# Storing q, k and v from ScalarE's queue in the first tiles of a fused attention layer

## The reference

```
xn = layernorm(x)
q, k, v = xn @ wq + bq, xn @ wk + bk, xn @ wv + bv      # 16 heads of 16
fq, fk = elu(q) + 1, elu(k) + 1
kv    = einsum('bhnd,bhne->bnde', fk, v)      # per row: summed over its 16 heads
k_sum = fk.sum over heads
attn  = einsum('bhnd,bnde->bhne', fq, kv) / (einsum('bhnd,bnd->bhn', fq, k_sum) + 1e-6)
x1 = x + attn @ wo + bo
out = x1 + gelu(layernorm(x1) @ fc_w + fc_b) @ proj_w + proj_b
```

## Time and profile before

| what | value |
|---|---|
| median of 3 runs | 701.37 us (699.54 to 701.44) |
| profiled execution, time | 700.69 us |
| profiled execution, span | 699.0 us |
| TensorE busy | 655.5 us, 94% of the span |
| VectorE busy | 503.0 us, 72% |
| ScalarE busy | 448.0 us, 64% |
| mean granted TensorE clock | 0.975 of full speed |

### The profile page before, as it was taken

How to read it: one execution, slowest core, us unless ns; L and a number is a source line. 1 busy time by engine, 2 the same in 40 slices (tenths; PEclk the granted TensorE clock), 3 DMA queues, 4 the chain that set the end, 5 groups by cost and what they waited for, 6 DMA issues and landing times.

```text
span 699.0 us, 17818 instructions
## 1 busy us (share of the span) xinstructions
PE 655.5 (94%) x6346; PEld 574.9 (82%) x6346; DVE 503.0 (72%) x1350; ACT 448.0 (64%) x895; POOL 369.8 (53%) x535
## 2 busy tenths in 40 slices
PE   7789999998789999999999999999999995899997
PEld 5569999975578898888888888888987772799997
DVE  7874756424578777868878778878766567799992
ACT  5676655513367787767767667776753663788882
POOL 5153664125456545465583764846545563357642
PEclk9879999999999999999999999999999995999999
DMA  7399897414766555544555455564442523567840
GB/s 263 112 296 315 276 304 256 144 46 111 108 105 105 95 78 91 103 85 72 109 82 121 83 89 129 70 113 89 87 82 40 180 92 92 172 218 219 246 161 30
DMA packets 284802, 95.60 MB, mean 137 GB/s; under 512 B 213988, under 2 KB 281664, under 8 KB 284714
## 3 DMA queue, kind: packets, MB, share of 16 engines
q1 hardware_dynamic: 267610, 82.27, 48.7%
q0 software_dynamic: 4992, 11.47, 5.9%
q10 hardware_dynamic: 12112, 0.72, 1.1%
HBM read 65.09 MB, written 29.40 MB: 135 GB/s over the span
## 4 chain that ended last, share of the span: by engine, by line
PE 55%; DVE 7%; issue 4%; POOL 4%; ACT 3%; SPq 2%; DMA 1%; ACTq 1%; POOLq 0%; DVEq 0%
PE bank L1932 49%; PE bank L1941 6%; POOL hids L901 2%; SPq L440 1%; DMA qkv_rows<-feats 1%; DVE den L1765 1%; DVE hn_ L1810 1%; DVE att_ L1763 1%; DMA keys<-qkv_rows 1%; DVE ots L1756 1%; DVE kv_ L1790 1%; POOL sth L886 0%; ACT feats L1125 0%; ACT L1201 0%; POOL stz L870 0%
## 5 line engine op out<-in xcount | busy, mean ns | idle before, releaser
L1932 PE MATMUL bank<-down_w,hids 128*128 128x256 f32 x768 | 104.5, 284 | 1.8 <-POOL hids L901 1.7
L1932 PE MATMUL bank<-hnts,up_w 128*128 128x512 f32 (+1 forms) x432 | 106.0, 382 | 0.1
L901 POOL TENSOR_TENSOR hids<-hid,hids 128x512 fp32r<-128x512 f32 (+1 forms) x68 | 83.3, 1226 | 36.0 <-ACT hids L1177 35.8
L1932 PEld LDWEIGHTS bank<-down_w,hids 128*128 128x128 f32 x768 | 96.6, 188 | 4.8 <-POOL hids L901 3.1
L1932 PE MATMUL bank<-qkv_w,xnts 128*128 128x256 f32 (+1 forms) x384 | 78.3, 352 | 1.5 <-DVE xnts L1776 0.9
L1932 PEld LDWEIGHTS bank<-hnts,up_w 128*128 128x128 f32 x432 | 71.2, 189 | 10.3 <-ACT hids L1177 0.3
L1932 PEld LDWEIGHTS bank<-qkv_w,xnts 128*128 128x128 f32 x384 | 61.7, 192 | 18.9 <-issue 5.8
L867 POOL TENSOR_SCALAR stz<-stz 128x1 f32<-128x1 f32 x32 | 7.2, 226 | 121.6 <-DVE stz L1794 121.6
L1172 ACT ACTIVATE hid<-bank,cols 128x512 f32<-128x512 f32 (+1 forms) x72 | 45.7, 640 | 39.4 <-PE bank L1932 38.0
L1932 PE MATMUL bank<-a_w,xa_h 128*128 128x256 f32 x256 | 60.2, 379 | 0.0
L1932 PE MATMUL bank<-xa_xt,a_w 128*128 128x256 f32 x384 | 55.1, 294 | 0.9 <-DVE xa_xt L1460 0.9
(11 more groups left out here) (292 smaller groups left out, 1562.1 us busy)
## 6 DMA issues: line engine op xcount, KB each, us to landing
qkv_rows<-feats SPq DMA_DIRECT2D x32, 384.0 KB, 3.1
a_raw<-in_L_ffn_w_dram SPq DMA_DIRECT2D x32, 256.0 KB
a_w<-in_L_ffn_w_dram SPq DMA_DIRECT2D x32, 256.0 KB
b_raw<-in_L_ffn_w_dram SPq DMA_DIRECT2D x32, 256.0 KB
b_w<-in_L_ffn_w_dram SPq DMA_DIRECT2D x32, 256.0 KB
mid_rows<-x_all SPq DMA_DIRECT2D x8, 512.0 KB
values<-qkv_rows SPq DMA_DIRECT2D x32, 128.0 KB
late_rows<-x_ SPq DMA_DIRECT2D x8, 512.0 KB, 3.1
```

Source lines behind the costliest of these rows:

```text
L901: pool.tensor_tensor(hids[1][u % 3][:, 0:w], hid[u % 2][:, 0:w], f32(hids[0][u % 3][:, 0:w]), ALU.subtract).then_inc(s_hidl, 1)
L1932: return pe.matmul(dst, left, right, start=start, stop=stop, skip_group_check=True)
```

## The change

ScalarE's queue issues the store of q, k and v for tiles 0 to 6, right behind its copy of v and behind a wait for the features; SyncE keeps the stores of the others. Step 6 joins the steps in which `qkv` stands ahead of `sum_kv` on TensorE, and on ScalarE ahead of `copy_kvt` and `help_keys`; `help_keys` stands ahead of `qkv` from step 7 instead of step 6.

```diff
-        QKV_FIRST = (4, 5)
+        QKV_FIRST = (4, 5, 6)
         HELPED = 7
+
+        def store_grids(engine, n):
+            i, rows = n % 2, slice(n * P, (n + 1) * P)
+            engine.wait_ge(s_feat, n + 1)
+            engine.wait_ge(s_val, n + 1)
+            engine.dma_start(qkv_rows[:, rows, :].rearrange("c p d -> p c d"),
+                             feats[i][:].rearrange("p (c d) -> p c d", c=3)).then_inc(s_grid[i], 16)
...
-            def store_grids(n):
-                i, rows = n % 2, slice(n * P, (n + 1) * P)
-                sp.wait_ge(s_feat, n + 1)
-                sp.wait_ge(s_val, n + 1)
-                sp.dma_start(qkv_rows[:, rows, :].rearrange("c p d -> p c d"),
-                             feats[i][:].rearrange("p (c d) -> p c d", c=3)).then_inc(s_grid[i], 16)
...
             for s in range(MID_STEPS):
-                if at(s, 2) is not None:
-                    store_grids(s - 2)
+                if at(s, 2) is not None and s - 2 >= HELPED:
+                    store_grids(sp, s - 2)
...
-                if 6 <= s < HELPED + 3:
+                if QKV_FIRST[-1] < s < HELPED + 3:
                     help_keys(s - 3)
                 if at(s, 2) is not None:
                     qkv(s - 2)
+                    if s - 2 < HELPED:
+                        store_grids(act, s - 2)
...
                 elif at(s, 5) is not None:
                     sum_att(s - 5)
+                if s == 6:
+                    qkv(4, v_free)
+                    v_free = (s_val, 5)
                 if at(s, 4) is not None:
                     sum_kv(s - 4)
```

## The result

| kernel | median, us | runs | ratio to before | 95% interval |
|---|---|---|---|---|
| before | 701.59 | 6 | 1 | |
| after | 706.08 | 6 (704.15 to 706.58) | 1.0049 | 1.0026 to 1.0072 |

The change makes the kernel 0.49% slower, 3.4 us by the ratio (1.8 to 5.0 by its interval); the two medians differ by 4.5 us. The profiled execution of after took 706.58 us, the longest of the six; its span is 704.9 us against 699.0. So its trace shows somewhat more loss than the median run has.

A forecast was written before the change was run, and what follows sets the result against it. TensorE is full from 245 us, so what the middle stage's start loses by step 8 stays: 0.37 (step 6) + 1.87 (steps 7 and 8) = 2.24 us, on the median 701.37, gives 703.6; range 699 to 706.5.

The forecast's parts named there:

- The signs that the prediction named: Among them: `turn_zn(2)` not before 172, `copy_o` behind the features, `ots` waits from 4.1 to about 6 us.
- Step 3: Loop step 3: store 1 and four key issues ahead of `turn_zn(2)` make it and TensorE 1.96 us later.
- Steps 4 to 7: TensorE 2.64 us later in step 4, 3.16 in step 5, 0.37 after step 6, 0.93 more in step 7.
- Step 6: Loop step 6: 4.8 us of stall and slow clock removed, TensorE 1.5 ahead; late `copy_kvt(2)` leaves 0.37 lost.
- Step 8: Loop step 8: wait, store and copy between features and `ots` make it 0.93 us later, as in step 7.
- The rival of the low clock: Gap before tile 2's q, k, v also brings low clock in step 4: 1.5 us more, 705.1; chance 0.13.
- SyncE's chain as the pace: Rival: SyncE's issues set the pace before step 6, ScalarE's lateness is absorbed; -2.9 us, 698.5; chance 0.22.
- Excluding issues: Rival: the two engines' DMA issues exclude one another, every store waits for one; +5.1 us, 706.5; chance 0.10.

The follow-up runs named there:

- the waits alone: Whole change, but stores stay on SyncE and ScalarE has only the waits for the features; 703.80 us, ratio 1.0031 to the kernel before.
- the order alone: Kernel before with only the new order of step 6, all stores on SyncE; 699.73 us, ratio 0.9967.
- stores alone: Kernel before with only the seven stores moved to ScalarE, step 6 in its old order; 706.88 us, ratio 1.0062.
- store last in 6 to 8: Whole change, but in steps 6 to 8 ScalarE's store stands behind that step's copies; 702.83 us, ratio 1.0014 to the kernel before.
- the last experiment: Kernel before, nothing changed, run again for a second profile; 701.29 us, ratio 0.9991.

## Why the prediction was right, and where it was off

- **Direction and mechanism.** Slower, by ScalarE's commands held behind the features: shown. Moving only the store's place takes the whole loss back (1.0049 to 0.9965), and the waits alone bring most of it (from 0.9967 for the order alone to 1.0031). The signs that the prediction named came: `turn_zn(2)` at 174.46, `copy_o` behind the features, waits for `ots` of 5.3 us in all, 1.2 and 1.0 longer in steps 7 and 8. The steps after 8 won back 0.46 us, which the prediction had at nothing.
- **Step 3.** From the end of the features of tile 1 to the copy of tile 2 I had 2.35 us (170.7 to 173.05); it is 2.80 (171.66 to 174.46), for the most part since the four key issues took 2.19 instead of 1.84. On TensorE the step fits: from q, k, v of tile 1 to those of tile 2 it takes 175.34 - 168.00 = 7.34 us, before 5.29, 2.05 more against the 1.96 forecast.
- **Steps 4 to 7.** Beside the low clock of step 4, the last column of the table moves by 0.43 us in all up to the projection of step 7.
- **Step 6.** The gain came. But I had counted 1.5 us of it as low clock near 191 that goes away. The second profile of before has none there, with nearly the same wait, so this credit holds for some executions and not for others. Without it the same working gives 3.7 instead of 2.24. How often the spell comes is open; by the mean clocks of the order alone it is not rare.
- **Step 8.** Between the projections of steps 7 and 8 TensorE takes 10.74 us, before 8.29, 2.45 more against the 0.94 forecast. The term itself is right: from q, k, v of tile 6 to the projection of step 8 it is 217.97 - 212.37 = 5.60 against 211.44 - 206.84 = 4.60, 1.00 more. The other 1.45 stands ahead of it and is mostly the low clock, which the sum had at nothing.
- **The rival of the low clock, given 0.13,** came true in the profile, and a second spell followed the gap of 2.34 us in step 7. The one of step 4 goes with the gap: in the four profiles in which TensorE waited over 2.0 us ahead of q, k, v of tile 2 (after, stores alone, store last in 6 to 8, waits alone: 2.58, 2.63, 2.60, 2.01) that product or the sum behind it is slow, in none of the eight others, whose gap is 1.28 or less. By these twelve profiles I gave it too little. In runs without a profile nothing shows where the clock fell.
- **SyncE's chain as the pace** falls: SyncE idles 19.0 us and the kernel is slower. The late stores on SyncE were what showed, not what set the time; issued earlier they gave nothing.
- **Excluding issues.** All seven stores on ScalarE took 0.377 to 0.383 us, and four of them were issued while SyncE was issuing too (171.70, 179.47, 187.37 and 195.57), so none shows a wait for SyncE. The lock that the Trainium skill describes (Perfetto Trace Analysis, "DMA Instruction — HWDGE (DVE, Sync)") is not seen on them. Some pairs of key issues did take 1.8 us with both engines issuing (1.82 at 198.01 in the order alone); why, no run settles.
- **Size.** 2.24 forecast, 3.4 measured (1.8 to 5.0); the median of after lies 0.4 us inside the upper end of the range. In the profile the low clocks of steps 4 and 8 make up what the forecast lacks from step 3 on. For the other runs this is not shown, and their mean clock speaks against it: 0.974 to 0.976 in the five others of after, 0.973 in the profiled one; in the kernel before 0.975 in the first profiled run and 0.974 as the mean of the twelve of the last experiment, on another chip. What is right in the size owes something to luck: the credit of 1.5 us for the clock near 191 us and the nothing for that of steps 4 and 8 have opposite signs.

## What to carry to other kernels

Here a DMA issue on ScalarE was cheap (0.38 us) and the wait ahead of it was not, because everything behind it in the engine's program waited too, and TensorE's gaps brought a low clock on top. Before a transfer is moved to another queue, list what stands behind it there and who waits for that; put it behind the work that others need, or on the engine whose next command waits for something later anyway. And take a change apart: here one half gained 0.33% and the other lost 0.62%. Compare with a second profile of the unchanged kernel before calling a spell of low clock its property.

## What was unexpected

- The same store takes 0.38 us to issue on ScalarE and 0.79 on GpSimd (0.90 at most), and the kernel with the slower issue is the faster of the two.
- The granted clock is part of the noise. Around 161 to 165 us it is low in one profile of the kernel before and full in the other, with some 1.3 us between the durations of the same product (3.69 against 2.36).
